# A new order of steps on every engine for a two-layer model of sixteen sequences

## The chip, the cores and the metric

The kernel runs on one core of a Trainium2 chip. The metric is device time in microseconds, the median of several executions. The core's engines are PE (TensorE, matmuls and transposes), DVE (VectorE), ACT (ScalarE), POOL (GpSimd) and SP (SyncE, which here only issues DMAs). Each engine has an instruction stream of its own; they meet through semaphores.

## The reference, cut to what matters

The input is 16 sequences of 512 tokens with 128 channels, f32. Two layers follow, each with a residual sum around a layer norm and a block:

```
layer 0, block:  in-projection to 2 x 256, causal 4-tap convolution, silu, softplus (delta)
                 for 16 states:  h_t = exp(delta_t * A) * h_(t-1) + x_t * x_t     (a scan over the 512 tokens)
                 sum over the states, D * x, gate silu(res), out-projection
layer 0, ffn:    8 experts; the gate is a softmax over minus the norms of the residuals of 8 projections,
                 the top 2 above 1/8 are kept and scaled to sum 1; experts' products are weighted and summed
layer 1, attn:   16 heads of 8 + 4 columns (the 4 rotary), causal softmax, values, out-projection
layer 1, ffn:    two ternary projections 128 -> 512, gelu(a) * b, two ternary layers 512 -> 512, one 512 -> 128
```

## The kernel before, in words

**Two phases.** Phase one takes each sequence through layer 0 and the attention of layer 1, phase two takes each through the last ffn. The residual stream (x_res) stays in SBUF throughout. Work on several sequences overlaps: while sequence b is in attention, b+1 is in the experts, b+2 in its scans and b+3 in its projections.

**Strands and places.** The stream of each engine is put together from strands. A strand is a Python generator for one kind of work on one sequence (`pe_scores(b)`, `dve_scans(b)`, ...), and each `yield` ends a step, a handful of instructions with their semaphore waits. `in_order` (L249) merges the strands of an engine by place: the next step issued is that with the smallest place. The place of step k of strand `name` of sequence b is `period * b + TIMES[name][k]`, plus a shift from `EDGES[name]` for the first three and last three sequences (`place`, L244; `EDGE_OF`, L241). Places look like nanoseconds but only their order counts. Phase one uses PERIOD, phase two F_PERIOD. In the kernel before, shifts are added in phase one alone (`edges=True`). The programs are built at L1375 to L1424 (phase one) and L1790 to L1839 (phase two). An engine runs its stream strictly in order, so a step that waits holds up all behind it.

**Steps that the text speaks of.**
- Scans. For 32 scans a sequence (2 channel tiles x 16 states), `act_decays` makes exp(delta * A) (ACT, L619), `dve_scans` scans (DVE, L634), `pool_sums` adds the states (POOL, L652 and L658). `pe_s_head` is the in-projection (PE, L511) and `act_s_head` holds the steps of convolution and silu (ACT, L528 to L548, L601).
- Experts. `pe_g_residuals` (PE, L714), squares (ACT, L762), sums (DVE, L798), the gate (DVE, with PE L723 and ACT L780), `pe_g_experts` (PE, L747), `dve_g_experts` (DVE, L882 and L892).
- Attention rows. `pe_t_proj` projects queries, keys and rotary parts (PE, L931 to L956). `act_t_proj` copies them (ACT, L975), DVE adds rotary parts (`dve_t_proj`, L997), and `sp_rows` (SP, L407 to L421) sends rows of them by DMA to the stacks, in which the rows of a head stand as the scores matmuls need them.
- Attention. A sequence has 20 scores steps, 0 to 19 (PE, L1076): two or four matmuls into one of two double PSUM banks (the trace counts each f32 matmul as two, here and below). `act_scores` takes the exponential (ACT, L1092) into one of two probability buffers, `pool_masks` zeroes what lies above the diagonal (POOL, L1124). `pe_values` has 14 steps: twelve groups of probabilities times values (PE, L1145), and as steps 9 and 13 two of transposes (L1155). Step 12 is the last group, four matmuls of 256 columns. `act_nums` (L1105) copies the sums out, `dve_values` divides, `pe_t_out` and `dve_t_out` close the block. Step 0 and step 10 of scores wait for the DMAs to the stacks.
- Between phases. `dve_f_first` starts phase two inside phase one's stream: its step 0 holds the scales (L1444, L1445) and the rounding of five ternary weight blocks (L1451, casts). `pe_bound` and `pe_f_first` belong to the same hand-over.
- Phase two. For each sequence the two ternary projections (PE, L1518 and L1523), tanh and products (ACT, DVE, POOL), hidden layers h1 (PE, L1545) and h2 (PE, L1569), out (L1589 and L1595). Every hidden operand is split into a rounded part (a cast on DVE, L1724 and L1737) and a remainder (a subtraction, half on DVE, L1727 for the second cell and L1740 for the third, half on POOL, L1766 and L1774; L1758 for the first cell).

Of the kernel before, what the change touches and what calls it, by code (L numbers as in the profile page):

```python
# [55 lines left out]
PERIOD, F_PERIOD = 72369, 31463  # L56
TIMES = {
    "act_decays": [-22525, -18696, -18581, -13661, -13661, -13194, -12414, -10439, -10233, -8343, -4602, -3209, 7447,
        8428, 9661, 10690, 12315, 14832, 17712, 19761, 23451, 24509, 25079, 25079, 29723, 34889, 35080, 36405, 36405,
        38870, 38870, 45179],  # L60
    "act_f_a": [96152, 99602, 103279, 104189, 104240, 119360, 122763, 127348],
    "act_f_first": [205950, 257282],
    "act_f_h1": [133868, 142633, 156837, 161646],
    "act_f_h2": [170674, 192800, 192800, 194618],
    "act_f_out": [247759],
    "act_f_rstd": [282068],
    "act_f_turned": [62867],
# [12 lines left out]
    "act_scores": [182268, 184363, 188398, 192545, 196181, 200731, 203486, 205289, 208841, 210344, 213421, 216672,  # L80
        219702, 226206, 231602, 236155, 241465, 242228, 247111, 251204],
    "act_setup": [-632324, -203455],
    "act_t_proj": [172334, 177009, 177605],
    "act_t_rstd": [140635],
    "act_t_setup": [-1923, 19968, 142865],
    "act_t_turned": [145233],
    "act_t_xn": [144196],
    "dve_bound": [213417],
    "dve_f_a": [94911, 106939, 110426, 121217],
    "dve_f_compare": [44422, 91810, 152629, 183399, 279564, 308311],  # L90
    "dve_f_first": [165839, 196471, 196471, 218728, 404306],
    "dve_f_flags": [364743, 377622],
    "dve_f_h1": [141339, 152321, 159961, 168286],
    "dve_f_h2": [188511, 193805, 200957, 201596],
    "dve_f_moments": [270219],
    "dve_f_norm": [40589, 61047],
    "dve_f_out": [257211],
    "dve_g_experts": [123123, 123225, 129952, 132971, 133231, 136522, 138266, 139841, 139889],
    "dve_g_gate": [104823, 107510, 107823, 110823, 111797, 114454, 115792, 115792, 115792, 115792, 116089, 116089,
        116113, 116152],  # L100
    "dve_g_norm": [81937],
    "dve_g_sums": [90729, 91176, 94933, 95099, 97703, 98190, 103179, 103633],
    "dve_s_head": [-55119, -37341, -11166, -4631],
    "dve_s_norm": [-166920],
    "dve_s_out": [37189, 71097, 77729],
    "dve_scans": [-15503, -13968, -13968, -5723, -40, 1618, 5615, 13618, 13851, 14173, 14173, 15830, 15830, 15911,
        15911, 16110, 19570, 23395, 23608, 26110, 27811, 28986, 30736, 34037, 36416, 43057, 44735, 45889, 49735,
        49865, 49865, 49891],
    "dve_setup": [-157473, -80247, -70357, -55723, -29218, -12520, -12463],
    "dve_t_norm": [142309],  # L110
    "dve_t_out": [269575],
    "dve_t_proj": [159145, 162872, 185005, 192411],
    "dve_values": [246691, 246691, 264621, 264621],
    "pe_bound": [298680],
    "pe_f_a": [111471, 114886, 129619, 134383],
    "pe_f_first": [249821, 419927],
    "pe_f_flags": [337428],
    "pe_f_h1": [146057, 149624, 163714, 167187],
    "pe_f_h2": [182334, 196914, 198520, 211199],
    "pe_f_out": [245188, 263265],  # L120
    "pe_f_turn": [59082],
    "pe_g_experts": [116253, 123574, 126963, 128613, 129129, 131786, 133163, 135887],
    "pe_g_own": [113013, 116800],
    "pe_g_residuals": [88744, 88744, 90909, 90988, 91723, 91775, 95759, 97582],
    "pe_g_setup": [-59952, -34171, -29675, 19854, 20060, 36383],
    "pe_g_turn": [83262],
    "pe_s_head": [-58237, -44258, -33701, -7850],
    "pe_s_out": [71538],
    "pe_s_turn": [-67475],
    "pe_scores": [181097, 182890, 186956, 190704, 197015, 199768, 202440, 204869, 206527, 211178, 214684, 216404,  # L130
        222325, 225623, 233879, 236295, 239526, 241309, 244433, 248816],
    "pe_setup": [-465088],
    "pe_t_out": [263024, 269117],
    "pe_t_proj": [152328, 160203, 169666, 173680, 178460, 181768],
    "pe_t_setup": [-39851, -6508, 56406],
    "pe_t_turn": [149472],
    "pe_values": [192290, 197677, 202552, 211571, 213907, 218823, 224262, 234732, 237166, 241057, 247043, 251517,
        251517, 257996],
    "pool_f_a": [46662, 46662, 58881, 68997],
    "pool_f_h1": [100231, 106497],  # L140
    "pool_f_h2": [133770, 153310],
    "pool_g_sums": [124290, 124528, 126627, 128950],
    "pool_masks": [185840, 193071, 197026, 206388, 208629, 215893, 220247, 226355, 237591, 244522, 247564, 249463],
    "pool_s_head": [-27989, -24477, -3256, -193, 7965, 23809],
    "pool_setup": [-219914],
    "pool_sums": [-6973, -1188, 430, 4729, 4729, 7334, 7334, 10674, 10674, 11745, 12513, 20864, 20864, 22199, 25926,
        27970, 28125, 28805, 30223, 32089, 34360, 34360, 40556, 40556, 41089, 43484, 46407, 46991, 52521, 53193,
        58931, 62092],
    "pool_t_proj": [164803],
    "sp_f": [1101621],  # L150
    "sp_loads": [-108307],
    "sp_rows": [326342, 331233, 334660, 336842, 353050, 364784],
    "sp_weights": [224596],
}
EDGES = {
    "act_decays": [864, -1184, 244, -137, -5, -44], "act_f_first": [-11195, 0, 18985, -243, -11066, 5159],
    "act_f_rstd": [0, -489, -191, 1570, 16951, 17820], "act_g_gate": [3015, 726, 57, 192, 195, 315],
    "act_g_rstd": [-1741, -141, -1176, -769, 555, -97], "act_g_setup": [-51799, -5076, -17733, 5361, 6858, 0],
    "act_g_squares": [57, -414, 221, -46, -109, 1474], "act_g_turned": [-1635, -153, -1796, -383, -129, 174],
    "act_g_xn": [-4752, -2072, -2672, -2840, 2143, -1406], "act_inputs": [2295, 1386, 2344, -711, 0, 967],  # L160
    "act_nums": [-1677, 182, -1128, -2939, -194, -1738], "act_s_head": [116, -2531, -3678, -220, -210, 100],
    "act_s_rstd": [-10336, -10761, -2145, -1435, 0, 1498], "act_s_turned": [-1054, 0, 0, 272, 95, 306],
    "act_s_xn": [9281, 11360, 873, 881, -195, 0], "act_scores": [0, 0, 0, 96, 0, 2043],
    "act_setup": [82837, 2129, 0, -35871, 8871, 41147], "act_t_proj": [2257, 404, 443, -663, -1911, -2920],
    "act_t_rstd": [-136, 0, -337, 209, 0, -1129], "act_t_setup": [-13081, -3494, 75, 753, -12098, 14901],
    "act_t_turned": [-80, 1207, 42, 3718, -198, 0], "act_t_xn": [-3492, -109, -1891, -1681, 0, 31],
    "dve_bound": [3166, -7314, -23445, 0, 5522, 48655], "dve_f_first": [10772, 3948, 0, 1964, -1775, 1952],
    "dve_f_moments": [787, 1350, 1159, 0, 7617, 2077], "dve_g_experts": [4439, -89, 127, -183, 240, -367],
    "dve_g_gate": [-198, -251, 137, 573, -724, 393], "dve_g_norm": [-1264, 3848, 2360, -1845, 819, 0],
    "dve_g_sums": [-2096, -1348, 0, -87, -971, -761], "dve_s_head": [4806, 78, 2658, -101, 0, 1872],  # L170
    "dve_s_norm": [0, 1051, -9858, -3156, 0, -2699], "dve_s_out": [217, 1382, 1192, 99, 123, -3736],
    "dve_scans": [-5625, -1185, 27, -300, -32, -469], "dve_setup": [-8713, -6339, -7013, -191, 14746, -4980],
# [68 lines left out]
EDGE_OF = {0: 0, 1: 1, 2: 2, NSEQ - 3: 3, NSEQ - 2: 4, NSEQ - 1: 5}  # L241


def place(period, name, b, k, edges):  # L244
    shift = EDGES[name][EDGE_OF[b]] if edges and name in EDGES and b in EDGE_OF else 0
    return period * b + TIMES[name][k] + shift


def in_order(period, strands, edges=False):  # L249
# [5 lines left out]
    while parts:  # L255
        part = min(parts)
# [1688 lines left out]
```

## Time and profile before

| | |
|---|---|
| median of 3 runs | 1606.09 us (1604.8 to 1608.68) |
| the profiled execution, its own time | 1609.73 us |
| its span, first to last instruction | 1608.2 us |
| mean granted TensorE clock | 0.959 |
| busy: PE, DVE, ACT, POOL | 1474.6, 1354.4, 1242.6, 1239.7 us |
| instructions | 23,773 |

Busy time is that of the engine's instructions by the profile; "idle before" is the time the engine stood still ahead of an instruction, with what released it. Phase one ends near 1250 us. Its steady part, in which all stages overlap, runs from about 220 to 1087 us. A granted clock of 1.00 is 2.4 GHz, the upper of TensorE's two levels; 0.50 would be the lower, 1.2 GHz.

### The profile page before, as it was taken

What the parts mean: (1) busy time and instruction counts of PE and PEld (TensorE: products, weight loads), DVE (VectorE), ACT (ScalarE), POOL (GpSimd) and SP (SyncE); (2) the same over time, 40 slices, a digit from 0 to 9 for tenths busy, and PEclk for the clock granted to TensorE, in tenths of its full rate; (3) what the DMA queues carried; (4) which work ended last, traced back from release to release, by engine and by line L of the source; (5) the groups of instructions that cost most, each with busy time, mean ns of one, the idle gap of its engine ahead of it and who ended that gap; (6) DMA issues with size and microseconds to landing.
All of it is one profiled execution on the core that took longest, in us unless ns stands there. A gap on an engine that the chain in (4) does not pass through costs nothing.

```text
span 1608.2 us, 23773 instructions
## 1 busy us (share of the span) xinstructions
PE 1474.6 (92%) x7687; PEld 789.1 (49%) x7687; DVE 1354.4 (84%) x2518; ACT 1242.6 (77%) x2144; POOL 1239.7 (77%) x1219
## 2 busy tenths in 40 slices
PE   4356799999999999999999999999989899999997
PEld 2123344444444444444444444434434688788885
DVE  5999899999999999999999999995431787977774
ACT  5875699999999999999999999995545555555542
POOL 4988799999999999999999999996232355555562
PEclk8676799999999999999999999999999899999999
DMA  4000000000000000000000000002000000000000
GB/s 157 1 0 0 20 1 21 4 18 21 1 20 5 17 12 10 20 1 21 5 17 21 1 21 4 17 15 79 21 11 10 1 1 14 14 14 14 8 20 29
DMA packets 14688, 27.59 MB, mean 17 GB/s; under 512 B 3981, under 2 KB 4566, under 8 KB 14042
## 3 DMA queue, kind: packets, MB, share of 16 engines
q1 hardware_dynamic: 14554, 25.98, 5.9%
q8 instruction: 62, 1.02, 0.3%
q14 instruction: 72, 0.59, 0.1%
HBM read 9.20 MB, written 4.19 MB: 8 GB/s over the span
## 4 chain that ended last, share of the span: by engine, by line
PE 45%; DVE 28%; ACT 16%; issue 5%; DMA 4%; POOL 1%; SPq 1%; ACTq 0%; DVEq 0%; POOLq 0%
DVE state_fast L634 14%; PE bank L1076 9%; PE bank L1569 7%; PE bank L1545 7%; ACT prob_fast L1092 5%; ACT state_fast L619 4%; PE bank L747 4%; DMA stacks_fast<-parts_fast 3%; PE bank L1145 3%; ACT bank L762 3%; PE bank L505 2%; DVE chan_all_kept L570 2%; PE bank L1589 2%; DVE own_fast L892 2%; PE bank L1518 2%
## 5 line engine op out<-in xcount | busy, mean ns | idle before, releaser
L634 DVE TENSOR_TENSOR_SCAN state_fast<-state_fast,bank 128x512 f32<-128x512 f32 x512 | 592.0, 1199 | 9.6 <-ACT bank L601 5.2
L658 POOL TENSOR_TENSOR sum_fast<-sum_fast,state_fast 128x512 f32<-128x512 f32 x384 | 480.4, 1275 | 11.2 <-DVE state_fast L634 11.1
L1092 ACT ACTIVATE prob_fast<-bank 128x1024 f32<-128x1024 f32 x320 | 325.4, 1018 | 94.7 <-PE bank L1076 80.2
L1076 PE MATMUL bank<-stacks_fast 64*128 64x512 f32 (+3 forms) x2048 | 365.1, 466 | 22.6 <-DMA stacks_fast<-parts_fast 13.4
L619 ACT ACTIVATE state_fast<-chan_all_kept,neg_a_fast 128x512 f32<-128x512 f32 x512 | 344.4, 713 | 9.1 <-POOL sum_fast L652 8.6
L1076 PEld LDWEIGHTS bank<-stacks_fast 64*128 64x128 f32 x2048 | 172.2, 187 | 217.6 <-ACT prob_fast L1092 107.1
L1124 POOL TENSOR_SCALAR_AFFINE_SELECT prob_fast<-prob_fast 128x512 f32<-128x512 f32 x256 | 169.4, 674 | 121.4 <-ACT prob_fast L1092 119.3
L1145 PE MATMUL bank<-prob_fast,v_ext_fast 128*32 128x512 f32 (+3 forms) x2048 | 172.5, 442 | 5.3 <-POOL prob_fast L1124 5.3
L1758 POOL TENSOR_TENSOR cell_a_fast<-th_fast,cell_a_fast 128x512 fp32r<-128x512 f32 x64 | 99.4, 1553 | 80.3 <-ACT cell_a_fast L1630 80.3
L747 PE MATMUL bank<-we_t_fast,xnt_g_fast 128*128 128x512 f32 x256 | 141.9, 651 | 2.8 <-DVE g_prod_fast L882 2.8
L714 PE MATMUL bank<-resid_m_fast,xnt_g_fast 128*128 128x512 f32 x256 | 133.8, 631 | 6.5 <-DVE gate_fast L798 5.1
L1545 PE MATMUL bank<-cell_a_fast,w_all_fast 128*128 128x512 f32 x512 | 129.1, 395 | 0.0
L1569 PE MATMUL bank<-cell_b_fast,w_all_fast 128*128 128x512 f32 x512 | 127.8, 393 | 0.0
L1545 PEld LDWEIGHTS bank<-cell_a_fast,w_all_fast 128*128 128x128 f32 x512 | 96.7, 189 | 21.9 <-issue 0.4
L1569 PEld LDWEIGHTS bank<-cell_b_fast,w_all_fast 128*128 128x128 f32 x512 | 96.0, 188 | 21.3
L1145 PEld LDWEIGHTS bank<-prob_fast,v_ext_fast 128*32 128x32 f32 x2048 | 48.5, 108 | 113.6 <-issue 95.7
L1704 DVE SCALAR_TENSOR_TENSOR th_fast<-th_fast,bank 128x512 f32<-128x512 f32 x64 | 43.8, 684 | 65.5 <-ACT th_fast L1624 65.5
L798 DVE TENSOR_REDUCE gate_fast<-bank 128x4 f32<-128x512 f32 x128 | 83.3, 679 | 17.9 <-ACT bank L762 17.7
L652 POOL TENSOR_TENSOR sum_fast<-state_fast 128x512 f32<-128x512 f32 x64 | 86.5, 1360 | 7.1 <-DVE state_fast L634 7.1
L1774 POOL TENSOR_TENSOR cell_c_fast<-full_fast,cell_c_fast 128x512 fp32r<-128x512 f32 x32 | 41.6, 1299 | 64.9 <-DVE cell_c_fast L1737 64.9
L1630 ACT ACTIVATE cell_a_fast<-th_fast 128x512 fp32r<-128x512 f32 x64 | 40.7, 635 | 64.1 <-DVE th_fast L1713 64.0
L1624 ACT ACTIVATE th_fast<-bank,s_half_kept 128x512 f32<-128x512 f32 x64 | 43.9, 687 | 55.8 <-PE bank L1518 55.7
(218 smaller groups left out, 2632.2 us busy)
## 6 DMA issues: line engine op xcount, KB each, us to landing
stacks_fast<-parts_fast SPq DMA_DIRECT2D x128, 64.0 KB
stacks_fast<-rest_fast SPq DMA_DIRECT2D x128, 32.0 KB
out_x<-f_out_fast SPq DMA_DIRECT2D x16, 256.0 KB, 2.0
x_res_kept<-in_x SPq DMA_DIRECT2D x1, 2048.0 KB, 14.3
chan_all_kept<-in_h_t SPq DMA_DIRECT2D x2, 1024.0 KB, 9.3
x_res_kept<-in_x SPq DMA_DIRECT2D x1, 1024.0 KB, 9.9
chan_all_kept<-in_w_t SPq DMA_DIRECT2D x3, 256.0 KB, 3.0
x_res_kept<-in_x SPq DMA_DIRECT2D x2, 256.0 KB, 3.3
```

The lines of the kernel that those rows point to most:

```text
L619: act.activation(self.state(b, i)[:], self.chan(b, ct)[1], ACT.Exp, scale=self.neg_a[:, i:i + 1]).then_inc(self.a_decay.sem)
L634: dve.tensor_tensor_scan(h[:], h[:], self.banks[0][:], 0.0, ALU.mult, ALU.add).then_inc(self.v_scan.sem)
L658: pool.tensor_tensor(part[:], part[:], self.state(b, i + 1)[:], ALU.add).then_inc(self.p_sum.sem)
L714: pe.matmul(banks[3 + half][:], xnt[:, k * P:(k + 1) * P], self.resid_m[:, half * 512:(half + 1) * 512], start=True, stop=True).then_inc(s ...
L747: pe.matmul(banks[3 + e % 2][:], xnt[:, k * P:(k + 1) * P], self.we_t[:, half * 512:(half + 1) * 512], start=True, stop=True).then_inc(sel ...
L1076: ins = pe.matmul(self.scores(b, step)[:, c:c + SEQ - P * kt], rows[:, 1, h // 2, P * kt:P * kt + P], rows[:, 0, h // 2, P * kt:SEQ], star ...
L1092: act.activation(self.probs[u % 2][:, i * 1024:(i + 1) * 1024], self.scores(b, 5 * g + n)[:], ACT.Exp, scale=SCALE).then_inc(self.a_prob.sem)
L1124: pool.affine_select(out=blocks, in_=blocks, compare_op=ALU.is_ge, fill=0.0, base=0, pattern=[[0, GROUP], [1, P]], channel_multiplier=-1). ...
L1145: ins = pe.matmul(bank[32 * j:32 * j + 32, P * kt:SEQ], v_ext[:, v:v + 32], self.probs[u % 2][:, c:c + SEQ - P * kt], start=(kt == 0 and g ...
L1545: ins = pe.matmul(banks[2 + mt % 2][:], w["h1_t"][:, c:c + P], self.f_a[s][k][:, i], start=(k + i == 0), stop=(k == MT - 1 and i == parts ...
L1569: ins = pe.matmul(banks[4 + mt % 2][:], w["h2_t"][:, c:c + P], self.f_h1[s][k][:, i], start=(k + i == 0), stop=(k == MT - 1 and i == parts ...
L1758: pool.tensor_tensor(cell[:, 1], th[:], cell[:, 0].bitcast(F32), ALU.subtract).then_inc(self.p_f_lo.sem)
```

## The change

All places are new: TIMES, PERIOD, F_PERIOD and EDGES. Each entry of EDGES has twelve values instead of six: six shifts and six stretches, the latter in thousandths of a step's distance from the strand's first step. They are applied in both phases now, to the first three and last three sequences. No instruction, semaphore wait, buffer or shape is different; the order of steps within the engines' streams is. The diff, cut to the code and to the tables of the strands that the text speaks of:

```diff
-PERIOD, F_PERIOD = 72369, 31463
+PERIOD, F_PERIOD = 72469, 34521
 TIMES = {
...
-    "dve_f_first": [165839, 196471, 196471, 218728, 404306],
+    "dve_f_first": [85596, 93149, 177194, 187402, 380088],
...
-    "dve_t_proj": [159145, 162872, 185005, 192411],
+    "dve_t_proj": [160042, 163991, 185411, 191404],
...
-    "pe_f_h1": [146057, 149624, 163714, 167187],
-    "pe_f_h2": [182334, 196914, 198520, 211199],
-    "pe_f_out": [245188, 263265],
+    "pe_f_h1": [123811, 128450, 136771, 145932],
+    "pe_f_h2": [167157, 175249, 185615, 187809],
+    "pe_f_out": [222437, 240958],
...
-    "pe_scores": [181097, 182890, 186956, 190704, 197015, 199768, 202440, 204869, 206527, 211178, 214684, 216404,
-        222325, 225623, 233879, 236295, 239526, 241309, 244433, 248816],
+    "pe_scores": [177958, 182020, 187836, 192043, 195427, 199489, 202053, 204585, 207023, 213989, 215720, 218644,
+        226977, 228840, 234114, 236511, 238353, 239963, 244467, 247232],
...
-    "pe_values": [192290, 197677, 202552, 211571, 213907, 218823, 224262, 234732, 237166, 241057, 247043, 251517,
-        251517, 257996],
+    "pe_values": [196945, 197416, 203546, 210642, 215227, 220873, 227491, 234772, 237768, 239806, 247174, 248951,
+        251649, 256175],
...
 }
 EDGES = {
...
-    "pe_scores": [70, 0, 42, 43, -479, -1266], "pe_setup": [1254, 13770, 749, 0, 8073, 31042],
...
+    "dve_f_first": [1335, -3427, -6182, 19257, 1986, 64926, -950, -104, 624, 0, -246, -394],
...
+    "pe_scores": [832, 73, 204, 0, -535, 944, -4, -7, 0, 0, 0, -24],
...
+    "pe_values": [1515, -385, -59, -497, -761, 1289, -24, 0, 0, 0, 0, 0],
...
 }
-def place(period, name, b, k, edges):
-    shift = EDGES[name][EDGE_OF[b]] if edges and name in EDGES and b in EDGE_OF else 0
-    return period * b + TIMES[name][k] + shift
+def place(period, name, b, k):
+    times, shift = TIMES[name], 0
+    if name in EDGES and b in EDGE_OF:
+        at = EDGE_OF[b]
+        shift = EDGES[name][at] + (times[k] - times[0]) * (EDGES[name] + [0] * 6)[6 + at] / 1000
+    return period * b + times[k] + shift
...
-            part[0], part[2] = place(period, name, b, k + 1, edges), k + 1
+            part[0], part[2] = place(period, name, b, k + 1), k + 1
```

An example of how the places make the order, PE around scores step 0 of sequence 8. Before, `pe_values` of 7 has step 11 and 12 both at 7 x 72369 + 251517 = 758100 and `pe_scores` of 8 has step 0 at 8 x 72369 + 181097 = 760049, so the values step comes first. After, step 12 is at 7 x 72469 + 251649 = 758932 and the scores step at 8 x 72469 + 177958 = 757710, so the scores step comes first.

## Rows read from the trace of the kernel before

**Rows 1.** Windows: us, then busy us (instructions) of each engine, PE's granted clock, DMA.
```profile
144.00:187.70 43.70, 29.79 (x76) 14.11 (x74) 41.48 (x76) 28.86 (x60) 36.97 (x29) 0.77 0.04 11
187.70:260.00 72.30, 70.21 (x368) 29.56 (x368) 64.61 (x119) 64.32 (x111) 62.89 (x66) 0.94 0.05 12
...
603.70:672.85 69.15, 67.53 (x383) 30.65 (x383) 67.50 (x131) 66.23 (x116) 65.66 (x68) 1.00 0.06 13
...
1367.00:1388.10 21.10, 21.05 (x95) 16.81 (x95) 19.80 (x28) 10.64 (x19) 13.02 (x8) 1.00 0.04 14
```

**Rows 2.** Timeline of PE: start, duration in us, line, tile, form, [idle before <-releaser].
```profile
259.98 1.13 PE L1076 MATMUL bank<-stacks_fast 64*128 64x512 f32 x4 [0.71 <-DMA stacks_fast<-parts_fast]
...
601.56 1.54 PE L1145 MATMUL bank<-prob_fast,v_ext_fast 128*32 128x384 f32 x24
603.69 1.13 PE L1076 MATMUL bank<-stacks_fast 64*128 64x512 f32 x4 [0.59 <-DMA stacks_fast<-parts_fast]
...
637.39 1.13 PE L1076 MATMUL bank<-stacks_fast 64*128 64x512 f32 x4
...
672.85 1.13 PE L1076 MATMUL bank<-stacks_fast 64*128 64x512 f32 x4 [1.09 <-DMA stacks_fast<-parts_fast]
...
947.54 1.13 PE L1076 MATMUL bank<-stacks_fast 64*128 64x512 f32 x4 [0.63 <-DMA stacks_fast<-parts_fast]
```

**Rows 3.** Tile view of stacks_fast, who waited for it: us, times.
```profile
  PE bank L1076: 13.4, 16
```

**Rows 4.** Timeline of ACT, the chain of one period.
```profile
624.08 1.02 ACT L1092 ACTIVATE prob_fast<-bank 128x1024 f32<-128x1024 f32 x1 [0.48 <-PE bank L1076]
...
638.57 1.03 ACT L1092 ACTIVATE prob_fast<-bank 128x1024 f32<-128x1024 f32 x1 [0.35 <-PE bank L1076]
...
667.50 0.58 ACT L975 ACTIVATE parts_fast<-bank 128x512 f32<-128x512 f32 x1
```

**Rows 5.** Timeline of PE, the form of values step 12 and the row behind it.
```profile
623.96 0.64 PE L1145 MATMUL bank<-prob_fast,v_ext_fast 128*32 128x256 f32 x8
624.53 1.12 PE L747 MATMUL bank<-we_t_fast,xnt_g_fast 128*128 128x512 f32 x2
```

**Rows 6.** Timeline of PE and of DVE before the first attention.
```profile
139.86 2.07 PE L511 MATMUL bank<-xnt_s_fast,w_in_fast 128*128 128x512 f32 x2 [1.56 <-DVE chan_all_kept L574]
...
143.67 0.35 DVE L892 SCALAR_TENSOR_TENSOR x_res_kept<-bank,gate_fast,x_res_kept 128x128 f32<-128x128 f32 x1 [1.11 <-PE bank L747]
```

**Rows 7.** Timeline of ACT and of DVE in sequence 0's attention.
```profile
196.79 0.59 ACT L780 ACTIVATE w9t_fast<-bank 9x512 f32<-9x512 f32 x1 [1.82 <-PE bank L723]
...
200.77 1.22 DVE L634 TENSOR_TENSOR_SCAN state_fast<-state_fast,bank 128x512 f32<-128x512 f32 x1 [4.04 <-ACT state_fast L619]
```

**Rows 8.** Timeline of POOL, DVE and PE around the rounding of the ffn weights.
```profile
1174.47 0.63 POOL L1124 TENSOR_SCALAR_AFFINE_SELECT prob_fast<-prob_fast 128x512 f32<-128x512 f32 x1 [2.83 <-ACT prob_fast L1092]
...
1184.39 5.09 POOL L1124 TENSOR_SCALAR_AFFINE_SELECT prob_fast<-prob_fast 128x512 f32<-128x512 f32 x3 [4.70 <-ACT prob_fast L1092]
...
1181.22 0.69 DVE L997 TENSOR_TENSOR rest_fast<-bank,rope_fast 68x512 f32<-68x512 f32 x1 [6.78 <-PE bank L931]
...
1185.04 3.36 DVE L1451 CAST w_all_fast<-chan_all_kept 128x512 fp32r<-128x512 f32 x5
...
1188.95 1.07 PE L1145 MATMUL bank<-prob_fast,v_ext_fast 128*32 128x384 f32 x16 [3.44 <-POOL prob_fast L1124]
```

**Rows 9.** Timeline of PE, the two longest waits ahead of a scores step 0.
```profile
1016.63 1.13 PE L1076 MATMUL bank<-stacks_fast 64*128 64x512 f32 x4 [1.31 <-DMA stacks_fast<-parts_fast]
...
1206.99 3.51 PE L1076 MATMUL bank<-stacks_fast 64*128 64x512 f32 x8 [1.98 <-DMA stacks_fast<-parts_fast]
```

**Rows 10.** Window behind the longest of them, columns as in rows 1.
```profile
1207.00:1212.00 5.00, 5.00 (x19) 2.12 (x21) 0.72 (x3) 2.05 (x2) 0.37 (x1) 0.66 0.27 62
```

**Rows 11.** Groups of DVE, 1262 to 1595: count, busy us, mean ns, idle before.
```profile
L1740 DVE TENSOR_TENSOR cell_c_fast<-full_fast,cell_c_fast 128x512 fp32r<-128x512 f32 x32 | 47.5, 1486 | 1.1
...
L1727 DVE TENSOR_TENSOR cell_b_fast<-full_fast,cell_b_fast 128x512 fp32r<-128x512 f32 x32 | 24.1, 754 | 1.1
```

More of the change, by code:

```diff
@@ new lines @@
+    "act_f_rstd": [281977],
+    "act_f_turned": [44984],
+    "act_g_gate": [104032, 104032, 106310, 113356, 117597],
+    "act_g_rstd": [74665],
+    "act_g_setup": [61979, 91574, 148978, 181071, 186344],
+    "act_g_squares": [83845, 84171, 88779, 89882, 92636, 95360, 100114, 100197],
+    "act_g_turned": [80748],
+    "act_g_xn": [75585],
+    "act_inputs": [-22926, 14931],
+    "act_nums": [238940, 255733, 263889],
+    "act_s_head": [-31120, -24986, -22505, -14655, -9165, -1929, 10706],
+    "act_s_rstd": [-160196],
@@ new lines @@
+    "act_s_turned": [-69182],
+    "act_s_xn": [-129603],
+    "act_scores": [182021, 184774, 188546, 193535, 198139, 200880, 204348, 205714, 206660, 208722, 211259, 214931,
+        220040, 225737, 233431, 236469, 241611, 244112, 247955, 251725],
+    "act_setup": [-731651, -299900],
+    "act_t_proj": [173955, 177033, 177033],
+    "act_t_rstd": [137642],
+    "act_t_setup": [13441, 47333, 124997],
+    "act_t_turned": [145361],
+    "act_t_xn": [140097],
+    "dve_bound": [149082],
+    "dve_f_a": [78143, 88593, 94849, 100139],
@@ new lines @@
+    "pe_setup": [-960522],
+    "pe_t_out": [263721, 266796],
+    "pe_t_proj": [156185, 161430, 168247, 174512, 175988, 181305],
+    "pe_t_setup": [-50891, 98136, 157084],
+    "pe_t_turn": [150771],
+    "pe_values": [196945, 197416, 203546, 210642, 215227, 220873, 227491, 234772, 237768, 239806, 247174, 248951,
+        251649, 256175],
+    "pool_f_a": [32925, 41574, 42856, 47159],
+    "pool_f_h1": [88858, 90896],
+    "pool_f_h2": [130611, 134611],
+    "pool_g_sums": [123040, 123930, 130459, 132042],
@@ L188 @@
+    "sp_weights": [-17592, 1340, -11775, -4336, -28469, 0, -844, 1431, -461, 0, 2855, -8],
 }
@@ L241 @@
 EDGE_OF = {0: 0, 1: 1, 2: 2, NSEQ - 3: 3, NSEQ - 2: 4, NSEQ - 1: 5}
-def place(period, name, b, k, edges):
-    shift = EDGES[name][EDGE_OF[b]] if edges and name in EDGES and b in EDGE_OF else 0
-    return period * b + TIMES[name][k] + shift
+def place(period, name, b, k):
[4 more added lines that the diff above has]
+    return period * b + times[k] + shift
 def in_order(period, strands, edges=False):
-    parts = [[place(period, name, b, 0, edges), rank, 0] for rank, (name, b, _) in enumerate(strands)]
+    parts = [[place(period, name, b, 0), rank, 0] for rank, (name, b, _) in enumerate(strands)]
     for _, _, strand in strands:
```

254 lines of the change are left out of this document (136 added, 118 removed).

## The prediction

> **What bounds the kernel now.** I read the windows first. In steady state, about 69 us for each sequence, every engine but SP is nearly full: in one period of 69.15 us PE is busy 67.53, DVE 67.50, ACT 66.23 and POOL 65.66 [rows 1]. Only an order that removes or adds a wait can change that period. From 144 to 187.7 us, before the first attention, PE is busy 29.79 of 43.70 us and the full engine is DVE (41.48); in phase two (from 1250 us) PE alone is full, 21.05 of 21.10 us in a period of one sequence [rows 1].
>
> Next, who waited for the stacks of queries and keys, and PE's timeline. The first scores step of every sequence starts just after a wait for a DMA. Sequence 1's starts at 259.98 and sequence 11's at 947.54 [rows 2]: 687.56 us for ten periods, 68.76 each, and every one of the sixteen starts ends such a wait (13.4 us in 16 of them [rows 3]). That gives a closed chain. From scores step 0 (603.69) to step 11 (637.39) PE runs almost without a gap; ACT then waits 0.35 us for step 11's exponential at 638.57, is dense until it copies the projected keys at 667.50; SP sends those rows to the stacks, and the landed rows release the next scores step 0 at 672.85 [rows 2, 4]. Whatever is added to PE between steps 0 and 11 lengthens each period; what stands just ahead of step 0 lies under the DMA wait and costs nothing. ACT's waits in the first half end with PE too (0.48 at 624.08 [rows 4]), so ACT has no clock of its own there that would swallow a delay.
>
> **The change part by part.** No instruction, wait or buffer changes, only the order of steps on each engine. Merging the strands by both tables, I find in phase one 414 of PE's 1101 steps in another place, 534 of 1341 on DVE, 658 of 1452 on ACT, 249 of 881 on POOL and 6 of 98 on SP; in phase two 166 of 239 on PE, 195 of 244 on DVE, 228 of 286 on ACT, 108 of 128 on POOL, none on SP. Most moves are past one or two neighbours in the middle of an engine's work. SP's six are row copies of sequences 14 and 15, whose sources ACT sets. These shuffles I cost at nothing: each engine does the same work ahead of each key step, to within 2.3 us on DVE for the first key projection (later) and 3.2 for the block's output (earlier), and buffers between engines cover that. What follows doesn't cancel.
>
> *Steady, PE.* Today the last group of probabilities times values of sequence b-1 (step 12 of the values strand) stands ahead of scores step 0 of b: the row at 601.56 [rows 2] holds it, and PE still waits 0.59 us for the DMA behind it. The new order puts it behind scores step 0 for b = 1 to 14. It is four matmuls of 256 columns, x8 in the trace's count; the same form started at 623.96 and the next row at 624.53 [rows 5], 0.57 us. It moves from the DMA's shadow into the dense part: the wait ahead of step 0 grows by 0.57, and so does the period. 14 x 0.57 = +8.0 us. On ACT the part between exponential 11 and the key copy holds the same steps in both orders; the copies of the number bank and the decays change places, at nothing, since each goes on at once. Ends: -4 us (of PE's 69.15 - 67.53 = 1.62 us of idle time in the period 0.5 is not the wait of 1.09 ahead of step 0 [rows 1, 2]; if half of that closes as well, 14 x 0.25, and another chain absorbs the 0.57), +9 (0.64, the full duration of that row, 14 times). I take +8, by the row.
>
> *Start.* DVE has hardly a gap before the first attention; what it idles from 144 to 187.7 is 2.2 us [rows 1], in small waits such as 1.11 at 143.67 for expert matmuls of PE, behind an in-projection that took PE 2.07 us at 139.86 [rows 6]. The new order puts expert steps 5 to 7 ahead of such in-projections. PE's granted clock is 0.77 there, so partly at its lower level of 1.2 GHz [rows 1]. I take -1; ends -5 (twice those 2.2 us, for the stretch before 144 as well) and +2 (residual steps of sequences 0 and 1 now stand ahead of the in-projections of 2 and 3).
>
> *Sequence 0's attention* (187.67 to 259.98, 72.3 us). One scan waits 4.04 us at 200.77 for ACT: the decay stood behind a copy that itself waited 1.82 us for PE at 196.79 [rows 7], and behind five other steps in ACT's order. The new order takes that decay ahead of the copy. The scan comes 3 us sooner, but PE is busy 70.21 of 72.30 us here [rows 1], so little reaches the end: -1; ends -3 (all of it) and +1.
>
> *Tail, phase one.* The rounding of the ffn weights (L1451, five casts, 3.36 us at 1185.04) stands behind the last key projection, and falls together with three masks on POOL that took 5.09 us from 1184.39 where one takes 0.63 [rows 8]. PE then waits 3.44 us for a mask at 1188.95 [rows 8]. In the new order the casts stand ahead of key projection 0, in DVE's idle 6.78 us before 1181.22, where POOL has a single mask at 1174.47 [rows 8]. The wait of 3.44 goes, and with it the slow matmuls behind such a wait (1.25 us for eight at 1206.99, worked out below [rows 9]); up to 0.7 comes back if that mask meets a cast: -4. Ends: 0 (the casts meet other masks, or hold up the projection) and -4.5. Late next is the exponential ahead of each mask.
>
> *Phase two.* The second hidden layer comes about a quarter to a whole period earlier on PE, and the flags step earlier by 0.25 us, under the output store. PE has no gap to lose (0.05 us a period [rows 1]). The fill's first steps and the drain's last ones stand in the order they had. 0; ends -0.5 and +4, the latter from DVE, below. Price of the covered moves if the cover goes: DVE has 21.10 - 19.80 = 1.30 us a sequence to spare [rows 1].
>
> Sum: -1 - 1 + 8 - 4 + 0 = +2 us. Against the profiled execution (span 1608.2, 1.5 outside it, 1609.73 in all) 1611.7. That execution lies 3.64 above the median of 1606.09, so 1608.1 on the scale of the runs. What a measurement tells from no change is 0.3%, 4.8 us.
>
> **The rivals.**
> *The period is not lengthened.* One step of the starts, 603.69 to 672.85, is 69.16 where the mean is 68.76 [rows 2], with the same order: more than this one chain is at work, and another that the new order shortens may pay for the 0.57. For: DVE is as full as PE. Against: sixteen waits for the same DMA. Then start, first attention and tail remain, -6: 1600. Chance 0.25.
>
> *The longer wait costs PE its clock (slower).* Ahead of scores step 0 PE will idle 0.57 us more. After 1.31 us of waiting, at 1016.63, the scores ran at their usual 1.13 us for four; after 1.98 us, at 1206.99, eight took 3.51 where two rows of four take 2.26, 1.25 us more [rows 9], and the window from 1207 to 1212 shows a granted clock of 0.66, so mostly the lower level [rows 10]. The wait at 672.85 (1.09) would become 1.7, the one at 1016.63 1.9 [rows 2, 9]. The mean of all is 13.4 / 16 = 0.84 [rows 3], so I count three that come between the two cases. If each loses 1.25 us, +4: 1612. The Trainium skill (TensorE: Matmul & The Clock Gate, What's actually happening) holds that the clock is halved after idle time and given back by activity; it is this rival's rule, and the row at 1206.99 agrees. Against: PE is busy over nine tenths of the time around these waits. It decides from a wait between 1.31 and 1.98 us on. Chance 0.09.
>
> *DVE and POOL block each other more (slower).* In phase two DVE's subtraction for the third cell took 1.486 us on average, the like one for the second cell 0.754, on operands of one shape [rows 11]: the one already loses time, by where it stands. If the new order makes both of the second cell's meet POOL, DVE pays 2 x 0.73 = 1.46 us a sequence, 0.16 over its 1.30 to spare; with 16 sequences, and the fill paying too, about +3. The same mechanism leaves the casts of the tail beside masks, so the 4 us isn't saved. 1608.1 + 3 + 4 = 1615. It decides from 1.30 us a sequence on. For: 195 of DVE's 244 steps there have another place. Against: POOL has 8 us to spare of 21 [rows 1]. Chance 0.20. The Trainium skill (SBUF — State Buffer, Who interferes with whom) states that DVE and GpSimd share a pair of ports, that a cast or a DVE instruction with two SBUF inputs can need it, and that whichever was issued first keeps the other fully out. By that rule the subtractions block each other wherever they overlap, which is this rival's case in full; the masks of 5.09 us beside the casts agree [rows 8].
>
> *Nothing that counts moves.* The step behind scores 0 costs no more than it did and the casts still meet masks: 1606. Chance 0.10.
>
> **How the numbers follow.** The forecast, 1608, has 0.36. Its own range, with the bounds of its terms taken as partly independent, is 1603 to 1613. Eight in ten of all cases lie from 1598 (the first rival with a better start) to 1617 (the rival of the ports with its bounds). Faster by over 0.3% (below 1601.3): two thirds of the first rival (0.17), and the forecast and the last rival with start and tail at their better ends (0.10): 0.27. Slower (above 1610.9): the rival of the ports, most of the clock's, and a fifth of the forecast: 0.33. Within: 0.40.
>
> **What would show it.** Right: scores step 0 of sequences 1 to 11 spaced 69.3 us instead of 68.76, the values step (x8) behind it, and the DMA wait ahead of it near 1.2 us instead of 0.6; the scan near 201 us without 4 us of waiting; masks near 0.63 us each beside the casts, and no 3.44 us wait on PE; PE without gaps in phase two. Wrong: a spacing at or below 68.8; a mask of several us; a second-cell subtraction of 1.5 us and PE idle after 1263; or another end to the wait ahead of step 0 than the DMA.

## The result and the profile after

The changed kernel takes 1621.7 us (median of 4 runs, 1617.98 to 1626.14) against 1606.7 for the kernel before: 0.9% slower, ratio 1.0094 with an interval of 1.0064 to 1.0125. Its profiled execution took 1626.14 us, with a span of 1624.6. The forecast was 1608, the range ended at 1617.

The page of the changed kernel, the first lines of its part 1, and two windows of it (columns as in rows 1: the steady part, and one stretch behind a scores step 0):

```profile
span 1624.6 us, 23772 instructions
...
PE 1474.9 (91%) x7687; PEld 789.6 (49%) x7687; DVE 1381.5 (85%) x2518; ACT 1248.0 (77%) x2144; POOL 1238.8 (76%) x1219
```

```profile
260.00:1017.00 757.00, 724.77 (x4092) 328.79 (x4090) 739.69 (x1376) 705.73 (x1228) 698.11 (x721) 0.99 0.05 11
...
680.20:685.00 4.80, 4.74 (x18) 1.24 (x20) 4.66 (x10) 2.84 (x4) 3.42 (x4) 0.64 0.35 67
```

With the same 2518 instructions DVE is busy 1381.5 us instead of 1354.4. An order alone can't add work, so some DVE instructions must have become longer, by 27 us on balance: the first thing to look up.

**Where the time went.** The closed chain of the prediction can be read in both traces by three rows a period: scores step 0 on PE, exponential 11 on ACT, the copy of the keys on ACT (L975, L1032 in the new kernel, whose lines are 57 further down). Here is one period of the changed kernel, sequence 5 to 6, from the timelines of PE and of ACT:

```profile
538.24 1.13 PE L1133 MATMUL bank<-stacks_fast 64*128 64x512 f32 x4 [1.51 <-DMA stacks_fast<-parts_fast]
...
573.06 1.03 ACT L1149 ACTIVATE prob_fast<-bank 128x1024 f32<-128x1024 f32 x1 [0.20 <-PE bank L1133]
...
604.11 0.58 ACT L1032 ACTIVATE parts_fast<-bank 128x512 f32<-128x512 f32 x1
...
608.94 1.22 PE L1133 MATMUL bank<-stacks_fast 64*128 64x512 f32 x4
```

Part by part, against the period of before that starts at 603.69 [rows 2, 4]:

| part of the chain | before | after |
|---|---|---|
| scores 0 to exponential 11 (PE) | 638.57 - 603.69 = 34.88 | 573.06 - 538.24 = 34.82 |
| exponential 11 to the key copy (ACT) | 667.50 - 638.57 = 28.93 | 604.11 - 573.06 = 31.05 |
| key copy to scores 0 (SP, DMA) | 672.85 - 667.50 = 5.35 | 608.94 - 604.11 = 4.83 |

The other periods of the eleven that start at sequences 1 to 11 read the same way: 34.8 to 35.0 in the first part (but for one, below), 30.9 to 31.2 in the second, 4.5 to 5.5 in the third. (The scores row at 608.94 shows no wait: the granted clock had fallen behind an earlier wait of 1.70 us, at 605.32, and slow matmuls filled the time until the DMA.) The part in which I expected 0.57 us more has none, and the one that I costed at nothing has 2.12 us more. What stands in it is one row of DVE. The timelines of the changed kernel, DVE, POOL and ACT at this place of the next period but one:

```profile
670.49 1.26 DVE L855 TENSOR_REDUCE gate_fast<-bank 128x4 f32<-128x512 f32 x2
671.78 2.70 DVE L874 TENSOR_SCALAR gate_fast<-gate_fast 128x32 f32<-128x32 f32 x1
...
670.76 2.50 POOL L715 TENSOR_TENSOR sum_fast<-sum_fast,state_fast 128x512 f32<-128x512 f32 x2
673.22 1.23 POOL L1181 TENSOR_SCALAR_AFFINE_SELECT prob_fast<-prob_fast 128x512 f32<-128x512 f32 x2
...
674.51 0.23 ACT L826 ACTIVATE gate_fast<-gate_fast 128x32 f32<-128x32 f32 x1 [2.09 <-DVE gate_fast L874]
```

and the same place in the kernel before:

```profile
665.29 1.26 DVE L798 TENSOR_REDUCE gate_fast<-bank 128x4 f32<-128x512 f32 x2
666.59 0.18 DVE L817 TENSOR_SCALAR gate_fast<-gate_fast 128x32 f32<-128x32 f32 x1
...
665.33 1.26 POOL L658 TENSOR_TENSOR sum_fast<-sum_fast,state_fast 128x512 f32<-128x512 f32 x1
667.29 1.22 POOL L1124 TENSOR_SCALAR_AFFINE_SELECT prob_fast<-prob_fast 128x512 f32<-128x512 f32 x2 [0.70 <-ACT prob_fast L1092]
```

L817 (L874 after) is the first step of the experts' gate: a maximum over 128x32 numbers, 0.18 us. Before, it is issued at 666.59, just when POOL's sum of 665.33 ends, and POOL then pauses 0.70 us for an exponential. After, POOL has two sums without a pause from 670.76 and two masks behind them, and DVE's small operation, issued at 671.78, lasts until about 674.5, where the masks end. ACT waits 2.09 us for it, with the key copy behind that wait in its queue. The view of this one line, of the changed kernel (ns: shortest, median, longest of 16), and who waited for it:

```profile
L874 DVE TENSOR_SCALAR gate_fast<-gate_fast x16: 151/2698/2874, 113.2 to 1161.7; 128x32 f32<-128x32 f32 x16
...
  ACT gate_fast L826: 27.1, 13
```

Summed over its 16 executions the operation takes 31.4 us where it took 2.8. So it alone makes up the 27 us; the other changes, in both directions, nearly cancel.

**The span, in a sum.** Scores 0 of sequence 0 comes at 183.69 instead of 187.67 (-4.0), sequence 0's attention takes 71.60 instead of 72.31 (-0.7), the eleven periods from there to sequence 12 take 780.70 instead of 756.65 (+24.05), the next 68.96 instead of 67.01 (+1.95), the next 61.66 instead of 62.09 (-0.4), the end of phase one to the first ffn matmul 96.82 instead of 104.71 (-7.9), and phase two 361.2 instead of 357.8 (+3.4). That is +16.4, the difference of the spans. Of the 24.05, 23.7 lie in the second part of the chain, where the gate's operation is (2.16 a period); the first part adds 0.9, with 1.5 from a slow clock in one period, and the third gives back 0.6.

**The clock.** Two periods have a long first part, 36.34 and 36.55 us instead of 34.82: those that start at sequences 7 and 12. They follow the two longest waits ahead of scores step 0:

```profile
680.26 1.55 PE L1133 MATMUL bank<-stacks_fast 64*128 64x512 f32 x4 [2.01 <-DMA stacks_fast<-parts_fast]
```

and 2.19 us at 1035.99. The window behind 680.2, shown above, has a granted clock of 0.64, so mostly TensorE's lower level of 1.2 GHz. Each of the two cost 1.5 to 1.7 us. But the length of a wait alone doesn't decide it. In this trace the clock was 0.66 in the 5 us behind a wait of 1.70 us at 605.3 and 1.00 behind one of 1.72 at 534.6. In two traces of the experiments below, the first of the changed kernel with its division steps moved, the second of the changed kernel with its values step moved, a longer wait left the matmuls at full speed and a shorter one didn't:

```profile
1035.92 1.13 PE L1133 MATMUL bank<-stacks_fast 64*128 64x512 f32 x4 [2.25 <-DMA stacks_fast<-parts_fast]
```

```profile
681.63 2.02 PE L1133 MATMUL bank<-stacks_fast 64*128 64x512 f32 x4 [1.65 <-DMA stacks_fast<-parts_fast]
```

### The profile page after: what moved, and what is told of

Read it like the earlier page. It is cut to its first block, busy times and chain, and to the rows that moved or that the text cites. A ratio compares the mean times of both kernels' runs of the same rounds, so it can differ in the third digit from the quotient of the medians.

```text
span 1624.6 us, 23772 instructions
## 1 busy us (share of the span) xinstructions
PE 1474.9 (91%) x7687; PEld 789.6 (49%) x7687; DVE 1381.5 (85%) x2518; ACT 1248.0 (77%) x2144; POOL 1238.8 (76%) x1219
## 4 chain that ended last, share of the span: by engine, by line
PE 47%; DVE 19%; ACT 14%; POOL 9%; issue 7%; DMA 2%; SPq 1%; ACTq 0%; POOLq 0%; DVEq 0%
PE bank L1133 11%; DVE state_fast L691 9%; PE bank L1626 6%; PE bank L1602 6%; PE bank L804 5%; PE bank L1202 4%; ACT prob_fast L1149 4%; POOL sum_fast L715 3%; ACT state_fast L676 2%; DMA stacks_fast<-parts_fast 2%; DVE gate_fast L855 2%; POOL prob_fast L1181 2%; PE bank L750 2%; PE bank L1646 2%; DVE gate_fast L874 2%
## 5 line engine op out<-in xcount | busy, mean ns | idle before, releaser
L1181 POOL TENSOR_SCALAR_AFFINE_SELECT prob_fast<-prob_fast 128x512 f32<-128x512 f32 x256 | 173.2, 690 | 129.6 <-ACT prob_fast L1149 129.5
L1202 PE MATMUL bank<-prob_fast,v_ext_fast 128*32 128x512 f32 (+3 forms) x2048 | 177.1, 447 | 1.7 <-POOL prob_fast L1181 1.5
L1815 POOL TENSOR_TENSOR cell_a_fast<-th_fast,cell_a_fast 128x512 fp32r<-128x512 f32 x64 | 93.7, 1477 | 50.7 <-ACT cell_a_fast L1687 50.7
L709 POOL TENSOR_TENSOR sum_fast<-state_fast 128x512 f32<-128x512 f32 x64 | 82.9, 1307 | 4.1 <-DVE state_fast L691 4.1
```

Source lines behind the costliest of these rows:

```text
L1181: pool.affine_select(out=blocks, in_=blocks, compare_op=ALU.is_ge, fill=0.0, base=0, pattern=[[0, GROUP], [1, P]], channel_multiplier=-1). ...
L1202: ins = pe.matmul(bank[32 * j:32 * j + 32, P * kt:SEQ], v_ext[:, v:v + 32], self.probs[u % 2][:, c:c + SEQ - P * kt], start=(kt == 0 and g ...
```

## The experiments

What had to be told apart: is the 2.70 us of L874 a block by POOL's use of SBUF, is it a late input, and which move brought it; does my step of 0.57 us exist; and what do tail and phase two owe to the order.

### The gate's two small operations write to PSUM

```diff
-        dve.tensor_scalar(ss, ss, LN_MIN, None, ALU.max).then_inc(self.v_g_a.sem)
+        dve.tensor_scalar(sp, ss, LN_MIN, None, ALU.max).then_inc(self.v_g_a.sem)
...
-        act.activation(ss, ss, ACT.Ln).then_inc(self.a_g_norm.sem)
+        act.activation(ss, sp, ACT.Ln).then_inc(self.a_g_norm.sem)
...
-        dve.tensor_scalar(col(4), kept, KEPT_MIN, None, ALU.max).then_inc(c.sem)
+        dve.tensor_scalar(self.banks[4][:, 64:68], kept, KEPT_MIN, None, ALU.max).then_inc(c.sem)
...
-        dve.reciprocal(col(5), col(4)).then_inc(c.sem)
+        dve.reciprocal(col(5), self.banks[4][:, 64:68]).then_inc(c.sem)
```

> The new order, unchanged, but the gate's two small tensor-scalar operations (L874, 128x32, and L915, 128x4) write to PSUM instead of SBUF. Theory A (the 2.70 us of L874 in the new order is DVE kept out of SBUF by back-to-back POOL operations): L874 takes 0.2 us in every period, exponential 11 to key copy falls from 31.07 to about 28.9, the period from 70.8 to 68.7, the whole by 24 to 27 us to about 1596. Rival B (L874's long duration is a late input, or DVE itself is simply full at this place): L874 or what follows it still ends where it did, period 70.8, 1621. Rival C (my values step in the dense part of PE sets part of the longer period): period 69.3, 1604.

Measured: 1595.55 us (1593.98 to 1597.83), ratio to the kernel before 0.9925 (0.9896 to 0.9955). The order is the new one, step for step. The line's view, and DVE and POOL at the same place as above:

```profile
L874 DVE TENSOR_SCALAR bank<-gate_fast x16: 176/195/195, 114.1 to 1134.8; 128x32 f32<-128x32 f32 x16
```

```profile
661.43 0.20 DVE L874 TENSOR_SCALAR bank<-gate_fast 128x32 f32<-128x32 f32 x1
...
662.75 1.87 DVE L735 SCALAR_TENSOR_TENSOR y_all_fast<-chan_all_kept,skip_d_fast 128x512 f32<-128x512 f32 x1
...
660.40 2.49 POOL L715 TENSOR_TENSOR sum_fast<-sum_fast,state_fast 128x512 f32<-128x512 f32 x2
662.86 1.22 POOL L1181 TENSOR_SCALAR_AFFINE_SELECT prob_fast<-prob_fast 128x512 f32<-128x512 f32 x2
```

POOL works without a pause as before it, from 660.40 to 664.08, and the gate's operation takes 0.20 us in the middle of that. It isn't a late input (rival B). The block moves on to L735, which has its inputs in SBUF and takes 1.87 us instead of about 0.73. The output projection's weight loads wait for that one, but the chain doesn't get longer by it: its second part is 28.82 us (28.94 before) and a period 754.46 / 11 = 68.59 us. Rival C, 69.3 a period, falls with it.

### Which move fills POOL's pause

First guess: two DVE steps (the division of the attention sums) that the new order puts ahead of scan 21 instead of behind it. Once put back in the new order, once moved in the kernel before:

```diff
-    "dve_values": [245461, 245461,
+    "dve_values": [246300, 246300,
```

> The new order, but the two DVE steps that divide the attention sums (values 0 and 1 of the sequence before) stand behind scan 21 again, as before, and not ahead of it: one place changed. Theory A: scan 21 and POOL's sum for it come 1 us earlier, POOL runs out of work as in the kernel before, L874 takes 0.2 us: period 68.7, about 1597. Rival D (several moves together fill POOL's pause): L874 keeps 1.3 to 2.7 us, period 70 to 70.8, 1612 to 1621.

Measured: 1622.82 us, ratio 1.010 (1.007 to 1.013). L874 keeps its median of 2.674 us.

```diff
-    "dve_values": [246691, 246691,
+    "dve_values": [246000, 246000,
```

> The kernel before, with those two steps moved ahead of scan 21 as in the new order. Theory A: L817 grows from 0.18 to 1.5 to 2.7 us in the steady periods, ACT waits for it, period 68.76 to 70 to 70.8: 1620 to 1630. Rival D: it stays 0.18, period 68.8, 1607.

Measured: 1606.11 us, ratio 0.9993 (0.9977 to 1.0009), L817 0.180 us. A miss twice: DVE's order isn't the cause. (Both outcomes are the rival's.) The two timelines of POOL above hold the answer. Before, POOL does one sum and then the masks of step 10, for which it has to wait 0.70 us; after, it does two sums and then the masks. By the tables: sum 19 of the sequence in its scans stood behind masks step 10 and stands ahead of it now, for all steady sequences. One place each way:

```diff
-    "pool_masks": [186093, ..., 236759, 244596, 250245, 251876],
+    "pool_masks": [186093, ..., 236759, 244596, 248400, 251876],
```

> The new order with one place of POOL changed: masks step 10 stands ahead of sum 19 again, as in the kernel before, so POOL pauses for the exponential just when L874 is issued. Theory A (a pause of POOL lets the gate's operation in; the new order filled it): L874 0.2 us, exponential 11 to key copy 28.9, period 68.7, about 1597. Rival D (the DVE order is to blame, or no single move is): L874 1.3 us or more, 1610 to 1622. L915 keeps its 0.95 us in both.

Measured: 1596.21 us (1594.83 to 1602.03), ratio 0.9945 (0.9926 to 0.9964). The time is theory A's. The line's view and POOL around it:

```profile
L874 DVE TENSOR_SCALAR gate_fast<-gate_fast x16: 156/338/520, 111.9 to 1132.9; 128x32 f32<-128x32 f32 x16
```

```profile
657.72 1.28 POOL L715 TENSOR_TENSOR sum_fast<-sum_fast,state_fast 128x512 f32<-128x512 f32 x1
659.41 1.22 POOL L1181 TENSOR_SCALAR_AFFINE_SELECT prob_fast<-prob_fast 128x512 f32<-128x512 f32 x2 [0.41 <-ACT prob_fast L1149]
```

The operation is issued at 658.70, waits for the rest of that sum and ends at 659.05: 0.34 us in the median, not 0.18, and the second part of the chain is 28.86. L915 keeps its 0.95 us, so that one costs nothing.

```diff
-    "pool_masks": [185840, ..., 237591, 244522, 247564, 249463],
+    "pool_masks": [185840, ..., 237591, 244522, 249300, 249463],
```

> The kernel before with the reverse change alone: masks step 10 behind sum 19 on POOL. Theory A: L817 takes about 2.7 us in the steady periods, period 70.8, 1606.7 to about 1630. Rival D: L817 stays below 1.3 us, 1607 to 1612.

Measured: 1632.26 us (1629.14 to 1636.79), ratio 1.0166 (1.0148 to 1.0184), from this one swap in the kernel before.

```profile
L817 DVE TENSOR_SCALAR gate_fast<-gate_fast x16: 151/1931/2820, 113.3 to 1160.8; 128x32 f32<-128x32 f32 x16
...
  ACT gate_fast L769: 22.6, 15
```

So the swap alone makes and unmakes the loss. The eleven periods take 20.8 us more than before, 17.8 of them in the second part; the median is 2 us above the end of the expected range. In this kernel L817 takes 1.26 to 1.32 us in five periods and 2.54 to 2.82 in eight. In the short ones it is issued just as POOL's second sum starts and comes in ahead of the masks; in the long ones it is issued during the first sum and comes in behind the masks. Why DVE is let in at one boundary between two POOL operations and not at another stays open.

A control, the kernel before with the gate's operations in PSUM, so that the gain of the first experiment can't be the edit's own:

> Control: the kernel before with the gate's two small operations writing to PSUM. There they take 0.18 and 0.17 us already, so nothing is to be had: 1607.9. Were it faster by several us, the gain of the PSUM version of the new order would not be the removed blocking alone.

Measured: 1604.03 us, ratio 0.9985 (0.9972 to 0.9998). By the medians 2 us are the edit's own, by the interval at most 4.5, of the 26 that the same edit gave the changed kernel. In the traces the eleven periods take 756.90 us with it and 756.65 without.

### The step of the prediction

```diff
-    "pe_values": [..., 247043, 251517, 251517, 257996],
+    "pe_values": [..., 247043, 251517, 253600, 257996],
```

> The kernel before with my predicted term alone: values step 12 behind scores step 0 on PE, for sequences 1 to 14. My prediction: 0.57 us a period more from scores 0 to exponential 11, 1607.9 to about 1615. Rival E (the delay is absorbed where PE and ACT wait for each other, or the step is shorter there): 34.90 stays, 1608. If it costs here but the new order as a whole shows 34.82, other moves of the new order pay for it.

Measured: 1617.93 us (1614.29 to 1620.41), ratio 1.0071 (1.0049 to 1.0092). The period from sequence 6 to 7 of it, PE and ACT:

```profile
606.83 1.13 PE L1076 MATMUL bank<-stacks_fast 64*128 64x512 f32 x4 [1.06 <-DMA stacks_fast<-parts_fast]
607.89 0.64 PE L1145 MATMUL bank<-prob_fast,v_ext_fast 128*32 128x256 f32 x8
...
642.21 1.03 ACT L1092 ACTIVATE prob_fast<-bank 128x1024 f32<-128x1024 f32 x1 [0.41 <-PE bank L1076]
```

The step stands behind scores 0 at 607.89, the first part is 642.21 - 606.83 = 35.38 us, 0.48 more than 34.90 in every steady period, and the wait ahead of scores 0 grew from 0.59 to 1.06. The periods from sequence 1 to 12 take 762.41 us, 5.8 more. Most of the rest of the loss is the end of phase one: the period of sequence 14 takes 64.98 us instead of 61.26. It holds the wait of 3.44 us that the kernel before has too, with slower matmuls behind it here, and ends in a wait of 2.52 us instead of 1.98; what of that is the move's I can't tell. The term exists, then, and nearly in its size (0.48 for 0.57). In the new order the first part is 34.82, so other moves of the new order pay for it.

In the changed kernel itself the same step is moved back:

```diff
-    "pe_values": [..., 248951, 251649, 256175],
+    "pe_values": [..., 248951, 248951, 256175],
```

> The new order, with values step 12 back ahead of scores step 0 on PE. My prediction's term: -0.57 us a period, the wait ahead of scores step 0 shrinks from 1.5 to 0.9, 1622 to about 1614. Theory A with the part from scores 0 to exponential 11 already at 34.82 against 34.90 before: it falls to about 34.3 at most if ACT follows, -0.4 a period; rival E (ACT and PE take turns there, and the gap closed elsewhere): nothing, 1621.

Measured: 1620.74 us, ratio 1.0086 (1.0053 to 1.0119). The first part falls to between 34.3 and 34.9 in ten of the eleven periods (35.92 in the one with the slow clock), 2.5 us in all; the second stays at 31.0 to 31.3; the third takes 2.2 us of it back. The medians differ by 1 us, within what the runs scatter.

### The rounding of the weights

The kernel with the mask ahead (1596.21), with the casts, and the step behind them, behind the key projections again:

```diff
-    "dve_f_first": [85596, 93149,
+    "dve_f_first": [96200, 96400,
```

> The new order with masks step 10 ahead of sum 19 (1596.2), and the rounding of the ffn weights behind the last key projections again. My prediction's term: +4 us, 1600, with a mask of several us beside the casts and PE waiting 3 us for it. If the shorter end of phase one (97 against 104.7 us from scores 0 of sequence 14 to the first ffn matmul) comes from the casts in full: +7 to +8, 1604. If from other moves: 1596.

Measured: 1603.74 us (1600.0 to 1609.13), 7.5 more than without it (6.6 by the two ratios to the kernel before, 0.9986 and 0.9945). POOL and PE of this kernel, then POOL of the changed kernel beside the same casts (1195.50, 3.36 us):

```profile
1182.72 4.51 POOL L1181 TENSOR_SCALAR_AFFINE_SELECT prob_fast<-prob_fast 128x512 f32<-128x512 f32 x2 [4.69 <-ACT prob_fast L1149]
...
1187.29 1.94 PE L1202 MATMUL bank<-prob_fast,v_ext_fast 128*32 128x384 f32 x16 [3.44 <-POOL prob_fast L1181]
...
1187.00:1195.00 8.00, 7.71 (x38) 2.79 (x39) 3.46 (x12) 2.18 (x3) 2.06 (x3) 0.60 0.08 18
```

```profile
1195.59 3.77 POOL L1181 TENSOR_SCALAR_AFFINE_SELECT prob_fast<-prob_fast 128x512 f32<-128x512 f32 x1 [1.89 <-ACT prob_fast L1149]
```

With the casts early a mask is blocked as well, for 3.77 us, but PE has other work and waits only 0.37 us for it (at 1199.41). With the casts late PE stands 3.44 us, and the window behind has a clock of 0.60: its rows of 1.07 and 1.13 us take 1.94 and 2.08. Phase one from scores 0 of sequence 14 on takes 103.7 us with the casts late and 96.8 with them early; before and after were 104.7 and 96.8. So the casts are nearly all of the tail's gain. (The profiled execution with the casts late lost another 2.7 us to a slow clock at 1080, well ahead of the casts; that isn't theirs.)

### Phase two, and the fastest version

Phase two's new order with phase one in the order of before:

> Phase one in the order of before, phase two in the new one. If the 3.4 us by which phase two is longer in the trace of after (361.2 against 357.8 from the first matmul of it) belongs to the order: 1610, first matmul to end 361. If it is the clock of that execution: 1606.7, 358. My prediction's term was 0.

Measured: 1609.08 us against 1607.88, ratio 1.0011 (0.9997 to 1.0024), and 358.5 us from the first ffn matmul to the end against 357.8. The 3.4 us of the changed kernel's profiled execution belong to that execution: its phase two had a mean granted clock of 0.96, that of the kernel with the gate in PSUM 0.98, and the kernels of the other experiments with the new phase two have 358.3 to 358.8.

The other way round, in the kernel with the gate in PSUM:

> The kernel with the gate's operations in PSUM (1595.6), with phase two in the order of before. If the order of phase two costs 3.4 us: about 1592. If not: 1595.6.

Measured: 1594.0 us (1593.84 to 1594.78) against 1595.55, ratio 0.9921 (0.9908 to 0.9934) against 0.9925. By the ratios that is 0.6 us, and 1.8 in the experiment before it: neither can be told from nothing.

Last, the values step in that kernel:

> The fastest so far (gate in PSUM, phase two in the order of before, 1594.0), with values step 12 ahead of scores step 0 on PE again. With nothing blocking the gate the term of my prediction can be read in the new order: alone in the order of before the step cost 0.48 us a period. If it costs that here too: scores 0 to exponential 11 from 34.82 to 34.35, 11 to 13 periods, -5 to -6, 1588. If the wait for ACT or the DMA takes its place: 1594.

Measured: 1591.84 us (1589.6 to 1593.08), ratio 0.9913 (0.9897 to 0.9929): the fastest, 15 us under the kernel before and 30 under the changed one. (Its interval overlaps with that of 1594.0, so the last 2 us aren't certain.) But the eleven periods take 753.68 us, only 0.6 less than in the kernel that it started from. PE ahead of scores 0 of sequence 6:

```profile
593.87 0.64 PE L1170 MATMUL bank<-prob_fast,v_ext_fast 128*32 128x256 f32 x8 [0.56 <-POOL prob_fast L1149]
594.43 1.13 PE L1101 MATMUL bank<-stacks_fast 64*128 64x512 f32 x4
```

The values step, ahead of scores 0 again, waits 0.56 us for its mask, and scores 0 follows it without a wait for the DMA. A second chain, over the last exponential and its mask, is now 0.1 us longer than the one over the DMA: in this period the first part is 34.69 (0.13 less), and the third, in most, 4.96 (0.12 more). Over the eleven the first fell by 2.0 and the third grew by 1.4. That is the outcome of rival E above, with the mask in the place of the DMA.

## Why the prediction was wrong

**What bounds the kernel**: right. The closed chain was the right place to read; the loss lies in it.

**The shuffles that I cost at nothing**: this is the step that failed. I compared how much work DVE has ahead of each key step, and wrote of the moves on all engines that they were past one or two neighbours and covered. One of them, POOL's sum 19 past masks step 10, fills a pause of 0.70 us in which DVE's 0.18 us operation got its turn, and makes that operation 2.70 us long. It costs 2.16 us in each of eleven periods, 23.7 us, shown by the swap in both directions. The amount of work ahead of a step was unchanged, as I said; its duration was not.

**Steady, PE**: +8.0 forecast, about 0 found. Alone in the kernel before, the step costs 0.48 us a period (0.57 forecast); in the new order the part it lies in isn't longer (34.82 against 34.88), and moving the step back there gains 0.2 to 0.6 us over eleven periods. Of the idle time inside this part, which I had only in the end of the range, some is gone: ahead of scores step 10 PE waits 0.18 us at 568.84 where it waited 0.43 at 634.25. Values step 3 stands ahead of scores step 9 now, which may be the reason; that wasn't tried. I hadn't added up such savings.

**Start and sequence 0's attention**: -1 and -1 forecast, -4.0 and -0.7 read. The -0.7 is the order's: 72.3 to 72.4 us in all six traces with phase one in the order of before, 71.4 to 71.7 in the eight with the new one. The -4.0 is in part scatter: scores 0 of sequence 0 comes at 184.09 to 187.91 in those six and at 180.72 to 184.62 in those eight. The middles lie 2 us apart, so 2 us for the order is an estimate; which wait it comes from isn't shown.

**Tail**: right in that the wait of 3.44 us goes, short in size. -4 forecast, -7.9 read, -6.6 to -7.5 by the experiment. The masks still meet the casts (3.77 us for one, where I named 0.63 as the sign of being right); what changed is that PE hardly waits for it. I had 3.44 for the wait and 1.25 for slow matmuls, read behind another wait, less 0.7 for such a mask. Behind the wait of 3.44 us itself the rows took 1.83, 1.08 and 1.49 us instead of 1.13, 0.64 and 1.13 in the kernel before, 1.5 us, and 2.3 in the experiment, at a clock of 0.60. With the 3.44 that is about what the experiment's period shows, 61.28 instead of 55.67. The other 2.3 us of the 7.9 lie behind scores 0 of sequence 15, 1.5 of them the slow matmuls at 1206.99 [rows 9].

**Phase two**: 0 forecast, +0.7 us in the traces, 0.6 and 1.8 by the ratios: not told from nothing. The subtractions changed places as the rival said, without a net cost. In the changed kernel:

```profile
L1784 DVE TENSOR_TENSOR cell_b_fast<-full_fast,cell_b_fast 128x512 fp32r<-128x512 f32 x32 | 35.8, 1118 | 1.1
...
L1797 DVE TENSOR_TENSOR cell_c_fast<-full_fast,cell_c_fast 128x512 fp32r<-128x512 f32 x32 | 33.0, 1031 | 1.1
```

Together 68.8 us where they were 71.6 [rows 11]; the casts ahead of them took 68.0 instead of 58.4. PE, which bounds this phase, hardly noticed.

**The rivals**: the one of DVE and POOL had the right mechanism and end (slower), with 0.20, and the wrong place. I looked for it where two long operations meet and asked whether DVE has spare time in phase two. It struck in the steady part, at the shortest operation on the chain. The rule of the Trainium skill that I cited there (SBUF — State Buffer, Who interferes with whom) names this case: a tensor-scalar can need the shared ports. The 2.70 us of L874 agree. That the same operation isn't held when it writes to PSUM is what the first experiment shows (0.20 us). The rival of the clock came true in two periods of twelve, for 3.2 us, at waits of 2.01 and 2.19 us, which the block had first made that long (1.51 and 1.71 in the kernel with the gate in PSUM). Its bound, a wait between 1.31 and 1.98 us, doesn't hold: matmuls kept their speed behind 2.25 and 2.09 us in other traces and lost it behind 1.65. Even my row at 1206.99 [rows 9] was one outcome of two. Of three other kernels with the order of before in this stretch, the same eight matmuls took 1.99 us in two (division steps moved; phase two alone) and 3.68 in one (gate in PSUM), behind the same wait of 1.98 or 1.99 us.

## What to carry to other kernels

Where DVE and POOL are both nearly full, an order is not only a sequence of durations. List the DVE operations on the critical chain that read and write SBUF alone, the shortest first, look at what POOL does in the moment of their issue, and protect the pause that lets them in, or give them a PSUM output so that they need none. A pause of an engine that is off the chain isn't free to be filled.

## What the runs showed of the hardware

A DVE tensor-scalar from SBUF to SBUF was kept out not for one POOL operation but through several that stood back to back: up to 2.87 us, over the rest of one sum, a second sum and two masks (and in five periods of one experiment over one sum only). The smallest was hit too: 128x4 numbers took 0.95 us instead of 0.17 in the steady periods (L915), off the chain. In the other direction a mask of 0.64 us took 3.77 beside five casts that followed each other (3.36 us). With a PSUM output the operation ran in 0.20 us beside the same POOL work. TensorE's clock did not follow the length of a wait: over the 5 us behind waits of 1.65 to 2.19 us the granted clock was 0.66 to 0.68 in some executions (1.65, 1.70, 1.98, 2.01, 2.19 us), and 1.00 behind 1.72, 2.09 and 2.25 us in others. A kernel that shows such a fall in one trace need not show it in the next.
